# The permutation's one-hots compared with repeated ranks, and the second flag inside the first pass, in a graph network kernel

## The reference

```
h = relu(layernorm(x))                      # first layer: two GCN convolutions
for W, b in ((W1, b1), (W2, b2)):
    norm = dinv[src] * edge_weight * dinv[dst]
    h = segment_sum((h @ W)[src] * norm, dst) + b     # relu between the two
x = x + log_softmax(h)
h = relu(layernorm(x))                      # second layer: GIN with edge features
aggr = segment_sum(relu(h[src] + edge_attr @ We + be), dst)
x = x + relu(batchnorm(relu((h + aggr) @ W1 + b1) @ W2 + b2))
```

## Time and profile before

| what | value |
| --- | --- |
| median of 3 runs | 7237.86 us |
| lowest and highest | 7178.89 and 7238.14 us |
| profiled execution | 7202.73 us |
| its span, from the first to the last instruction | 7200.9 us |
| mean granted TensorE clock of it | 0.786 of full speed |
| TensorE busy | 4929.8 us, 68% |
| VectorE busy | 3687.3 us, 51% |
| GpSimd busy | 3762.4 us, 52% |
| ScalarE busy | 1294.4 us, 18% |
| gathers (L645) | 3476, 1036 ns each |
| permutation's one-hots (L1637) | 608, 749 ns each, 424.7 us |
| permutation's matmuls (L1149) | 2432, 428 ns each, 665.9 us |

### The profile page before, as it was taken

How to read it: one execution, slowest core, us unless ns; L and a number is a source line. 1 busy time by engine, 2 the same in 40 slices (tenths; PEclk the granted TensorE clock), 3 DMA queues, 4 the chain that set the end, 5 groups by cost and what they waited for, 6 DMA issues and landing times.

```text
span 7200.9 us, 123340 instructions
## 1 busy us (share of the span) xinstructions
PE 4929.8 (68%) x29893; PEld 3663.6 (51%) x29894; DVE 3687.3 (51%) x11918; ACT 1294.4 (18%) x4290; POOL 3762.4 (52%) x3554
## 2 busy tenths in 40 slices
PE   4566666666666766667666666667777777777777
PEld 4444444444444545555555555555555555555554
DVE  3565666666666554444444444464444444444444
ACT  4211111111111230000000000042222222211113
POOL 2477777777777544444444444454333433344444
PEclk5577777777777667777777777768888888888888
DMA  1122222221222121111111111132222222222223
GB/s 42 46 46 48 46 46 49 46 48 46 46 49 46 48 49 40 40 37 38 42 40 40 37 38 41 42 90 62 55 54 54 56 54 55 55 51 52 51 52 99
DMA packets 239971, 355.98 MB, mean 49 GB/s; under 512 B 68655, under 2 KB 137178, under 8 KB 239545
## 3 DMA queue, kind: packets, MB, share of 16 engines
q0 software_dynamic: 111232, 170.85, 12.8%
q1 hardware_dynamic: 128688, 184.55, 8.1%
HBM read 315.83 MB, written 39.30 MB: 49 GB/s over the span
## 4 chain that ended last, share of the span: by engine, by line
PE 57%; DVE 22%; issue 10%; POOL 4%; DVEq 4%; ACT 2%; DMA 1%; ACTq 0%; POOLq 0%; SPq 0%
PE psum L1202 29%; PE psum L1126 10%; PE psum L1149 8%; DVE rows_g L1594 5%; POOL rows_g L645 4%; DVE x_tab L1587 3%; DVE hot L1553 3%; DVE x_tab L1637 2%; PE psum L1197 2%; DVE hot L1556 2%; PE psum L1134 1%; DVEq L426 1%; PE psum L1070 1%; PE psum L1138 1%; DVE x_tab L1632 1%
## 5 line engine op out<-in xcount | busy, mean ns | idle before, releaser
L645 POOL DMA_INDIRECT rows_g<-table,idx x3476 | 3599.5, 1036 | 3149.1 <-ACT idx L782 2100.9
L1202 PE MATMUL psum<-x_tab 125*128 x12160 | 2080.8, 342 | 607.5 <-DVE rows_g L1594 474.8
L1202 PEld LDWEIGHTS psum<-x_tab 125*128 125x128 bf16 x12160 | 1406.1, 116 | 1258.9 <-issue 645.6
L1564 DVE TENSOR_TENSOR acc<-acc,psum 96x128 f32 x1173 | 328.3, 280 | 2703.9 <-PE psum L1126 2699.7
L1126 PE MATMUL psum<-hot,rows_g 128*96 128x128 f32 x7512 | 1112.1, 300 | 60.0 <-DMA rows_g<-table,idx 43.8
L1126 PEld LDWEIGHTS psum<-hot,rows_g 128*96 128x96 f32 x7512 | 1029.0, 185 | 197.8 <-issue 95.5
L1149 PE MATMUL psum<-x_tab 128*104 128x512 bf16 x2432 | 665.9, 428 | 530.3 <-DVE x_tab L1637 530.3
L780 ACT ACTIVATE attr<-edge 128x12 f32 (+1 forms) x1173 | 243.8, 208 | 3875.0 <-PE psum L1126 3875.0
L1553 DVE TENSOR_SCALAR hot<-iota,attr 128x128 f32<-128x128 f32 x2504 | 694.0, 356 | 81.7 <-issue 38.8
L1149 PEld LDWEIGHTS psum<-x_tab 128*104 128x104 bf16 x2432 | 323.5, 141 | 808.5 <-ACT x_tab L825 322.2
L1587 DVE TENSOR_SCALAR x_tab<-x_tab 125x512 bf16<-125x512 bf16 x3040 | 653.4, 288 | 38.8 <-ACT x_tab L799 38.8
(11 more groups left out here) (251 smaller groups left out, 3441.8 us busy)
## 6 DMA issues: line engine op xcount, KB each, us to landing
x_tab<-sorted_keys SPq DMA_DIRECT2D x304, 250.0 KB
rows_g<-table,idx POOLq DMA_INDIRECT x3476, 2.5
x_more<-in_edge_attr_dram SPq DMA_DIRECT2D x238, 64.0 KB, 1.9
sorted_attr<-x_tab SPq DMA_DIRECT2D x38, 384.0 KB, 3.0
x_more<-sorted_attr SPq DMA_DIRECT2D x152, 96.0 KB
table<-x_tab SPq DMA_DIRECT2D x13, 840.0 KB
x_tab<-in_edge_attr_dram SPq DMA_DIRECT2D x38, 256.0 KB, 2.8
x_tab<-in_x_dram SPq DMA_DIRECT2D x2, 4200.0 KB
```

Source lines behind the costliest of these rows:

```text
L645: pool.indirect_dma_start(out=rows_g[u][0:np_, g * F:(g + 1) * F], out_offset=None, in_=table[p], in_offset=bass.IndirectOffsetOnAxis(ap=i ...
L1202: last = pe.matmul(ps_sel[c], mask[j][:, c * P:(c + 1) * P], tab3[:, bass.ds(w[c] + j, 1), :, :].rearrange("q a k f -> q (a k f)"), start= ...
L1564: dve.tensor_tensor(a, a, ps_agg[t.b], ALU.add).then_inc(fast.added, 1)
```

## The change

The rank of each edge is copied 16 times side by side into `rank_h`, in half precision, as a fourteenth link of the chain in `sort_rank`. The one-hots of the permutation are then made by an instruction with two tensors, `tensor_tensor` with `is_equal`: the numbers 0 to 2047 seen as 128 runs of 16, against the 16 equal ranks of the column, which are read again for each run. Before it was `tensor_scalar`, with one tensor and the rank as a scalar.

The second flag gets a tile of its own, `flag2_i`. TensorE's sum of `bad` and VectorE's three small instructions stand behind the loop of pass 0, ahead of its last eleven groups, where TensorE waits for the sort's end and for the copied keys. The waits for `s_edge` and `s_gathers` are gone. All engines read the new flag behind pass 0 too, where they read the first one before; only the degrees use `flag_i`. Each engine waits for `s_flag2` before that reading.

```diff
--- before.py
+++ after.py
@@ -138,6 +138,7 @@
         bank_f = sb("bank_f", [P, 3, CH])
         flag_f = sb("flag_f", [1, 1])
         flag_i = sb("flag_i", [1, 1], I32)
+        flag2_i = sb("flag2_i", [1, 1], I32)
         iota = sb("iota", [P, SW])
         ident = sb("ident", [P, P])
         w_c = sb("w_c", [F, 2, F])
@@ -197,6 +198,7 @@
         ship = at_tab.take(SC * PF, BF16).rearrange("p (c k) -> p c k", k=PF)
         ea_out = at_tab.take(SE, BF16)
         key_T = at_tab.take(P)
+        rank_h = at_tab.take(SC * 16, F16).rearrange("p (c k) -> p c k", k=16)
         tot_sb = at_tab.take(P)
         dupes, rank, blk_s, dst_s, wgt_s, start_s, key_s, miss, rel_s, far_s = [at_tab.take(SC) for _ in range(10)]
         same = at_tab.take(SC * SC).rearrange("p (c d) -> p c d", d=SC)
@@ -320,7 +322,6 @@
         s_eat = [sem(f"sorted_attr_loaded{k}") for k in range(2)]
         s_zin = sem("z_part_loaded")
         s_slow3 = sem("slow_attr_loaded")
-        s_gathers = sem("first_pass_gathered")
 
         class Ring:
 
@@ -403,9 +404,9 @@
         def last_steps(ahead=0):
             return [Step(ITERS - 1, k) for k in range(ahead, REST)]
 
-        def if_far(eng, sweep):
-
-            any_far = eng.value_load(flag_i[0:1, 0:1], min_val=0, max_val=1)
+        def if_far(eng, sweep, flag=flag2_i):
+
+            any_far = eng.value_load(flag[0:1, 0:1], min_val=0, max_val=1)
             with eng.If(any_far > 0):
                 sweep()
 
@@ -711,11 +712,9 @@
                             gather(fast, p, t.s, t.u, EP, fast_got[t.u])
                 for t in last_steps():
                     gather(fast, p, t.s, t.u, t.np_, fast_got[t.u])
-                if p == 1:
+                if p == 0:
                     pool.wait_ge(s_flag2, 1)
                 if_far(pool, lambda: each_slow(pool, lambda s, np_: gather(slow, p, s, 0, np_, slow_got[p])))
-                if p == 0:
-                    pool.sem_inc(s_gathers, 1)
 
             pool.wait_ge(s_xt, 64)
             pool.wait_ge(s_logz, 1)
@@ -907,6 +906,7 @@
                 act.activation(we3[:, k, :], we_rest[:, :], ACT.Copy).then_inc(s_we3, 1)
             stage_first(0)
             sort_pass()
+            act.wait_ge(s_flag2, 1)
             if_far(act, lambda: sweep(0))
             act.wait_ge(s_sorted, LOOPS)
             act.wait_ge(fast.agg, U + NS)
@@ -926,7 +926,6 @@
             for c, k in SPLIT:
                 split_part(1, c, k)
             stage_loops(1, select_part)
-            act.wait_ge(s_flag2, 1)
             if_far(act, lambda: sweep(1))
 
 
@@ -1087,7 +1086,7 @@
                     last.then_inc(far_dsum, 1)
                 each_slow(pe, one)
 
-            if_far(pe, deg_sweep)
+            if_far(pe, deg_sweep, flag_i)
             zero_deg(False).then_inc(s_dall, 1)
             pe.wait_ge(s_dsb, 1)
             for c in range(CA):
@@ -1276,18 +1275,18 @@
             pe.wait_ge(s_lf, 1)
             pe.matmul(ps_least_b, ones_row[:, :], least_f[:, :], start=True, stop=True).then_inc(s_lb, 1)
             sort_pass()
+            pe.wait_ge(s_sorted, LOOPS)
+            pe.wait_ge(s_keyc, LOOPS + 1)
+            pe.matmul(ps_bad, ones_col[:, :], bad[:, :], start=True, stop=True).then_inc(s_bad, 1)
             end_pass(0)
+            pe.wait_ge(s_flag2, 1)
             if_far(pe, lambda: sweep(0))
 
-            pe.wait_ge(s_sorted, LOOPS)
-            pe.matmul(ps_bad, ones_col[:, :], bad[:, :], start=True, stop=True).then_inc(s_bad, 1)
             pe.wait_ge(s_par, 16 * 11)
             LAG = 3
             for q in range(NQ + LAG):
                 if q < NQ:
                     linear(0, q)
-                if q == LAG:
-                    pe.wait_ge(s_flag2, 1)
                 if q >= LAG:
                     if (q - LAG) % 2 == 0:
                         pe.wait_ge(s_relu, ((q - LAG) // 2 + 1) * JQ)
@@ -1500,7 +1499,7 @@
                     last.then_inc(far_deg, 1)
                 each_slow(dve, one)
 
-            if_far(dve, deg_sweep)
+            if_far(dve, deg_sweep, flag_i)
             then(dve.memset(deg_sb, 0.0))
             dve.wait_ge(s_dall, 1)
             dve.tensor_copy(deg_sb[:, 0:NA], ps_degf)
@@ -1602,7 +1601,7 @@
                     dve.wait_ge(s_part3, part_n(p, c, k))
                     dve.tensor_tensor(t, t, tab3[:, js, k, :], ALU.subtract).then_inc(s_left3, 1)
 
-            LINKS = 13
+            LINKS = 14
             links = [0]
 
             def link(it, ins):
@@ -1631,10 +1630,13 @@
                 link(it, dve.tensor_tensor(prod, blk, ps_rank.unsqueeze(2).to_broadcast([P, J, SC]), ALU.mult))
                 link(it, dve.tensor_reduce(rank[:, :], prod.rearrange("p j c -> p c j"), AX.X, ALU.add))
                 link(it, dve.tensor_tensor(rank[:, :], rank[:, :], dupes[:, :], ALU.add))
+                link(it, dve.tensor_copy(rank_h, rank[:, :].unsqueeze(2).to_broadcast([P, SC, 16])))
 
             def sort_perm(it, c):
                 dve.wait_ge(s_permd, SC * it + c + 1)
-                dve.tensor_scalar(perm[c % 3], iota_h, rank[:, c:c + 1], None, ALU.is_equal).then_inc(s_perm, 1)
+                split16 = lambda t: t.rearrange("p (a k) -> p a k", k=16)
+                dve.tensor_tensor(split16(perm[c % 3]), split16(iota_h),
+                                  rank_h[:, c, :].unsqueeze(1).to_broadcast([P, SE // 16, 16]), ALU.is_equal).then_inc(s_perm, 1)
 
             def sort_columns(it):
                 e = edge2[:, bass.ds(it * NP, NP), :]
@@ -1695,7 +1697,12 @@
                         if k == 9:
                             sort_end(it)
                     assert links[0] == LINKS
+                dve.wait_ge(s_bad, 1)
+                then(dve.tensor_reduce(bad_f[:, :], ps_bad, AX.X, ALU.max))
+                then(dve.tensor_scalar(bad_f[:, :], bad_f[:, :], 0.5, None, ALU.is_ge))
+                dve.scalar_tensor_tensor(flag2_i[:, :], flag_f[:, :], float(W), bad_f[:, :], ALU.is_ge, ALU.max).then_inc(s_flag2, 1)
                 end_pass(0)
+                dve.wait_ge(s_flag2, 1)
 
             def sort_prepare():
                 ai, bi = prep_a.bitcast(I32), prep_b.bitcast(I32)
@@ -1854,13 +1861,6 @@
             sort_prepare()
             sort_pass()
             if_far(dve, lambda: sweep(0))
-            dve.wait_ge(s_bad, 1)
-            then(dve.tensor_reduce(bad_f[:, :], ps_bad, AX.X, ALU.max))
-            then(dve.tensor_scalar(bad_f[:, :], bad_f[:, :], 0.5, None, ALU.is_ge))
-            dve.wait_ge(s_edge, 1)
-            dve.wait_ge(s_gathers, 1)
-            then(dve.scalar_tensor_tensor(flag_i[:, :], flag_f[:, :], float(W), bad_f[:, :], ALU.is_ge, ALU.max))
-            dve.sem_inc(s_flag2, 1)
             dve.wait_ge(s_eas, 16 * (LOOPS + 1))
             dve.wait_ge(s_keyd, 16 * (LOOPS + 1))
             dve.wait_ge(s_par, 16 * 11)
```

## The result

The change makes the kernel **slower by 5.7%**: 7638.55 us, the median of 4 runs (7605.49 to 7644.28), against 7231.36 (7178.89 to 7238.14); ratio 1.057, 95% interval 1.051 to 1.063. The forecast was slower too, at 7383 and up to 7540: the sign was right, but at +180 us the size was less than half of the +407 measured.

A forecast was written before the change was run, and what follows sets the result against it. It took the first-pass loop's chain VectorE to TensorE and back as the bound, POOL an almost equal second. Loop 194, end of pass -15, flag +1 made +180 on 7202.7: 7383 us, range 7290 to 7540.

The forecast's parts named there:

- The one-hots: First pass, L1637 on VectorE: 608 comparisons in two-operand form take 1.236 us each instead of 0.743.
- a warm step: First-pass loop, step with three one-hots at full clock: 5.75 us between additions instead of 4.82.
- Step 3: First-pass loop, step that starts at half clock: only its first one-hot counts, +0.49 us.
- step 2: First-pass loop, step with one one-hot: +0.45 us for it and +0.45 for the new copy of the rank.
- steps 4 to 6: First-pass loop, among the four alike steps 4 to 7 with three one-hots: +0.93 us each.
- The chain alone: VectorE to TensorE and back in the first-pass loop: 61.4 us an iteration, +5.1, so +194 us over 38.
- The flag: Column sum and VectorE's small instructions ahead of the pass's last steps: +1.3 there, at most 0.2 back, together +1 us.
- POOL at nothing: First-pass gathers: POOL needs 50 to 61.5 us an iteration, stays beside the chain's 61.4, costed at 0.
- the 228 us that might come back: First-pass gathers: delays put at 1564 x 0.146 us, which POOL would regain if two-operand comparisons held nothing.
- The end of the pass: Last groups after the sorting: with POOL ahead, TensorE waits less for gathers, -15 us, at most -20.
- POOL was the bound after all: Rival, first-pass loop: the chain followed POOL, which is freed of delays, giving 7075 us; 7%.
- The clock's case: Rival: TensorE falls to half clock inside three-one-hot steps, 7510 us for one of four, 7890 for all; 13%.

The follow-up runs named there:

- paused_again: Kernel after, but VectorE waits for each one-hot of a burst to finish before starting the next, in a set without delays: 7502.03 us, single run.
- port_ahead: Kernel after with one-source one-hots read as 5 rows of 410, the first of steps 3 to 7 built earlier: 7163.85 us, 0.9911 of the kernel before.
- after_ahead: Kernel after with the first one-hot of steps 3 to 7 built ahead of the step's window one-hot and addition: 7388.39 us, single run.
- flag_only: Kernel before with only the new second flag, old one-source one-hots kept: 7858.93 us, 1.0011 of the kernel before, slowed set.
- one_port: Kernel before with the new flag and one-source one-hots read as 5 rows of 410, written as 2 of 1025: 7785.91 us, ratio 0.9998, slowed set.
- after_again: The kernel after, unchanged, run again in a slowed set: 8037.78 us, 1.0322 of the kernel before.
- hots_only: Kernel before with only the two-operand one-hots and repeated ranks, old flag kept: 8075.67 us, 1.0293 of the kernel before, slowed set.
- first_ahead: Kernel before with the new flag and the first old one-hot of steps 3 to 7 built earlier: 7765.29 us, ratio 0.9975, slowed set.
- wait_between: Kernel after, but VectorE waits for each one-hot of a burst to finish before starting the next, slowed set: 7887.99 us, 1.0132 of the kernel before.

## Why the prediction was wrong

**The one-hots: right.** 1.236 us forecast, 1.215 measured; a warm step 5.75 forecast, 5.83 measured. Step 3 grew by 0.41 (forecast 0.49), step 2 with the copy by 0.71 (forecast 0.90), steps 4 to 6 by 1.01 each (forecast 0.93), by the medians of the distances between additions. POOL's part shows in steps 7 and 8, which grew by 2.66 and 2.83. The chain alone needs 61.5 an iteration: 38 x (61.5 - 56.3) = 198 us, against 194. It was right step by step, so this is not luck.

**The flag: right.** +1 forecast, 0 to 0.2% in its own kernel.

**POOL at nothing: the step that failed.** The prediction said "Two-operand comparisons hold gathers up too" and put it at worst as "two gathers held for a whole comparison in five steps", 50 + 5 x 2 x 1.15 = 61.5 us. Both factors were wrong. It is one gather for each burst, and it is held to the burst's end: 4.29 us instead of 0.94 in the row shown, 3.35 more. Five bursts make 16.7, and 50 + 16.7 = 66.7 us is POOL's iteration, which is the 66.5 measured. (Summed over all gathers of the loop, the time above 0.94 is 16.7 us an iteration too, and 6.1 before.) That was 5.0 above the chain: 38 x 5.0 = 190 us which stand nowhere in my sum. The row that should have told me stood in the earlier trace rows: 2.57 us for a gather beside the burst of 2.08 is the whole burst, not one comparison of 0.75. It began at 1240.62 and ended 0.12 behind this burst:

```profile
1241.00 2.07 DVE L1637 TENSOR_SCALAR x_tab<-x_tab 128x2048 bf16<-128x2048 f16 x3
```

I used that row only for the 228 us that might come back. Instead I took L1616's 1.38, a comparison that stands alone, and the 1.80 beside L1603, where one gather did pass with each subtraction. With 190 for it and 15 at the end of the pass instead of -15, my sum would have been 7202.7 + 194 + 190 + 15 + 1 = 7603, above my range and 0.5% from the median measured.

Beside the row stood the page "SBUF — State Buffer" of the Trainium skill (Who interferes with whom), which infers that a two-operand operation does not stall the making of descriptors. The trace disagrees more than I had said: 4.29 us beside two-operand one-hots, against 0.94 for a gather that nothing holds. Of VectorE's modes that use both ports, the same section says that whoever issues first gets the shared pair "for the whole instruction". The traces show more, with one source as with two operands: a gather held to the end of three instructions that follow one another without a pause (2.57 and 4.29 us, and 7.25 in the slowest form).

**The end of the pass: wrong in sign.** -15 forecast, +14.7 measured. It hung on POOL being ahead at the end of the loop, so it fell with the step above. Where POOL isn't late, the gain is there: the last ten groups take 13.2 us in paused_again and 13.8 in port_ahead.

**The rivals.** "POOL was the bound after all" named the right engine, and I priced it as freed. The clock's case (7510) did not come in the kernel after: between 1257.5 and 1275.0 us the granted clock is at full in the longer steps. It came in part where the pauses made the steps longer still, in steps 5 and 7 of paused_again (0.77).

**What stays open.** Why the subtractions of L1603, two operands and back to back, let a gather through with each, while the one-element one-hots, which are as long and as close, let none: the operands differ in type (float32 against 16-bit), and no run changed that alone. It is open, too, at which moments a burst of one-source one-hots holds a gather (last section), and why the 5.7% of the first result are 2.9 and 3.2% in the two slowed sets. Neither is it known what slowed the sets in which the kernel before took 7849 and 7792 us (last section).

## What to carry to other kernels

When an instruction on VectorE grows, look up what the longest gather beside it cost and compare that with the whole run of such instructions, not with one of them: its price on POOL is the burst's length for one gather. Two engines within a few per cent of one another (here 56.3 us for an iteration of the chain, and 40 x (1.089 + 0.30) = 55.6 for POOL) must both be costed, each with its own sum. And what holds a gather can be chosen: with the first one-hot of a burst started one place earlier, a form of the comparison that is slower by 0.5 us but holds nothing beat the kernel before by 0.9%, and the old form by about 1.5%.

## What the runs showed of the hardware

Beside the two-operand one-hots, a gather that has begun just ahead of a burst isn't held (0.94 at 0.09 us ahead, after_ahead); one that begins 0.02 into it is held to its end. A pause of about 0.2 us on VectorE is enough to let one in.

The one-source one-hots of the kernel before do it otherwise. In its loop the 100 gathers that began 0.15 to 0.54 us ahead of a burst were held until 0.12 behind its end (2.34 to 2.73 us), and the 166 that began inside one took 1.37 at most. In flag_only, with the same one-hots, 78 gathers that began 0.88 into a burst were held as well (2.00 to 2.34). So whether a gather is held depends on the moment at which the two meet, and by another rule in either form; the rule itself is not shown.

A one-source comparison of 2050 16-bit elements takes 1269 ns with its source in 5 separate rows, whether it is written as 2 rows or in one run, against 743 for 2048 in one run.

In two of the four sets every kernel was slower in all three passes (the kernel before by 8%). In the traces of those sets VectorE and ScalarE see TensorE's work late, in some places by 5 us and more, as in this row of one_port, where the trace names nothing on this core that ended the wait:

```profile
1007.81 0.28 DVE L1563 TENSOR_TENSOR acc<-acc,psum 96x128 f32 x1 [9.90 <-remote]
```

Counted where an addition of the first pass begins over 1 us after TensorE's aggregation has ended, there were 80 such delays (694 us together) in the kernel after (after_again), 91 (682) in hots_only, 71 in flag_only and in first_ahead (400 and 465), but 40 (133) in wait_between and 38 (123) in one_port, whose gathers are not held; one at most with few gathers, and none in the other two sets. The same chip ran one set with them and one without. They go with the gathers; what they are is not known.
